# Expert network of a 16-layer model: token rows gathered tile by tile through an inverted map in place of 16 scatters before the tile loop

## The reference, cut to what matters

```python
x = x + _L2_ffn_ref(_layernorm(x, axis=-1), gate_w, gate_b, w1, b1, w2, b2)

def _L2_ffn_ref(x, gate_w, gate_b, w1, b1, w2, b2):     # 8 experts, 128 -> 512 -> 128, TOP_K = 2
    xt = x.reshape(b * s, h)
    probs = jax.nn.softmax(xt @ gate_w + gate_b, axis=-1)
    _, idx = jax.lax.top_k(probs, TOP_K)
    one_hot = jax.nn.one_hot(idx, NUM_EXPERTS, dtype=xt.dtype)
    mask = (one_hot.sum(axis=1) > 0).astype(xt.dtype)
    h1 = jax.nn.relu(jnp.einsum('th,ehf->etf', xt, w1) + b1[:, None, :])
    out_e = jnp.einsum('etf,efh->eth', h1, w2) + b2[:, None, :]
    out = jnp.einsum('eth,te->th', out_e, mask)
    return out.reshape(b, s, h)
```

## Time and profile before

| | |
|---|---|
| median of 3 runs | 2968.0 us (2967.19 to 2973.27) |
| the profiled execution's own time | 2966.24 us |
| its span, first to last instruction | 2964.7 us |
| busy: PE / DVE / ACT / POOL | 77% / 61% / 47% / 29% |
| mean granted clock of PE | 0.902 of full speed |
| DMA: all / POOL's own queue (q0) | 80.91 MB / 10.76 MB |
| the four expert stages, first to last instruction | 840.8 to 943.7, 1064.4 to 1166, 2315.7 to 2419, 2543.7 to 2646 us |

### The profile page before, as it was taken

One profiled execution on the slowest core, in us unless ns is written; L12 is line 12 of the kernel. 1 busy time (PEld: TensorE's weight loads), 2 busy tenths in 40 slices (PEclk: granted clock), 3 DMA queues, 4 the chain that ended last, 5 costly groups with the idle time before them and its releaser, 6 DMA issues. The chain is left out here.

```text
span 2964.7 us, 36677 instructions
## 1 busy us (share of the span) xinstructions
PE 2295.0 (77%) x12494; PEld 1086.6 (37%) x12494; DVE 1800.1 (61%) x3201; ACT 1393.2 (47%) x2324; POOL 858.3 (29%) x852
## 2 busy tenths in 40 slices
PE   6678879999757757777766787799997578577777
PEld 2222344544336226223222223445443452362232
DVE  5959565554525725885559595655455357259855
ACT  5535536555423434545455355366544234346454
POOL 3721151000224433651037211500001243336410
PEclk9998989999869878999989989999998687789999
DMA  3002000000021221000000020000000311210000
GB/s 140 0 18 67 10 1 9 1 1 1 1 96 52 71 96 36 0 0 1 9 8 0 27 60 7 1 9 1 1 1 1 99 60 59 96 36 0 1 2 14
DMA packets 58912, 80.91 MB, mean 27 GB/s; under 512 B 10784, under 2 KB 38944, under 8 KB 58464
## 3 DMA queue, kind: packets, MB, share of 16 engines
q1 hardware_dynamic: 49376, 63.81, 6.7%
q0 software_dynamic: 4992, 10.76, 1.1%
q10 hardware_dynamic: 4352, 3.94, 0.5%
HBM read 53.83 MB, written 26.08 MB: 27 GB/s over the span
## 5 line engine op out<-in xcount | busy, mean ns | idle before, releaser
L2227 ACT ACTIVATE L1b_pr<-ps,L1b_mneg 128x512 f32<-128x512 f32 x256 | 173.5, 682 | 191.3 <-DVE L1b_mneg L2268 191.3
L2266 DVE TENSOR_REDUCE L1b_m<-ps 128x2 f32<-128x1024 f32 x128 | 156.7, 1225 | 88.7 <-PE ps L2117 83.5
L96 ACT ACT_TABLE_LOAD x44 | 56.5, 1283 | 286.7 <-PEq L495 64.8
L1478 POOL TENSOR_TENSOR L0a_db<-L0a_du,L0a_bs 128x1024 f32<-128x1024 f32 x64 | 150.5, 2360 | 106.9 <-DVE L0a_du L1589 61.9
L1478 POOL TENSOR_TENSOR L3a_db<-L3a_du,L3a_bs 128x1024 f32<-128x1024 f32 x64 | 150.4, 2359 | 106.0 <-DVE L3a_du L1589 59.5
L1901 ACT ACTIVATE L0b_pt<-ps 128x1024 f32<-128x1024 f32 x128 | 125.6, 1022 | 97.3 <-PE ps L1801 97.2
L1989 DVE TENSOR_REDUCE L0b_mx<-ps 128x1 f32<-128x512 f32 x256 | 157.9, 682 | 20.3 <-PE ps L1788 17.7
L2292 DVE COPY L1b_prt<-ps 128x512 f32<-128x512 f32 x128 | 88.5, 691 | 126.4 <-PE ps L2130 126.1
L267 POOL CAST L1g_xc<-xn 128x512 bf16<-128x512 f32 x2 | 1.5, 731 | 558.5 <-DVE xn L142 558.5
L1606 DVE TENSOR_TENSOR_SCAN L3a_hs<-ps,L3a_db 128x1024 f32<-128x1024 f32 x64 | 146.0, 2282 | 5.3 <-ACT ps L1398 5.3
L1606 DVE TENSOR_TENSOR_SCAN L0a_hs<-ps,L0a_db 128x1024 f32<-128x1024 f32 x64 | 146.0, 2281 | 4.2 <-ACT ps L1398 4.2
(11 more groups left out here) (697 smaller groups left out, 5293.0 us busy)
## 6 DMA issues: line engine op xcount, KB each, us to landing
L2f_wall<-expert_dram SPq DMA_DIRECT2D x32, 256.0 KB, 5.6
L2g_wall<-expert_dram SPq DMA_DIRECT2D x32, 256.0 KB
weights<-w_dram SPq DMA_DIRECT2D x5, 941.5 KB, 14.1
L0b_qs<-stack_dram SPq DMA_DIRECT2D x32, 96.0 KB, 2.2
stack_dram<-L0b_cut SPq DMA_DIRECT2D x24, 128.0 KB, 2.1
L2b_qs<-stack_dram SPq DMA_DIRECT2D x32, 96.0 KB, 2.2
stack_dram<-L2b_cut SPq DMA_DIRECT2D x24, 128.0 KB, 2.2
L2f_xg<-slots SPq DMA_DIRECT2D x10, 288.0 KB, 4.7
```

Of the source, the lines that this page charges most:

```text
L1478: pool.tensor_tensor(db[:, n % DEEP, :, :], du[:, b, :, :], bcast(bs[:, n % DEEP, :], 1, 2), ALU.mult).then_inc(input_ready, 1)
L2227: act.activation(pr[:, s % 2, h, :], g.ps[:, 2 * (s % 2) + h, :], ACT.Exp, bias=mneg[:, s % 2, h:h + 1], accum_out=total[:, u % 2, t, h:h ...
L2266: dve.tensor_reduce(m[:, s % 2, :], g.ps[:, 2 * (s % 2):2 * (s % 2) + 2, :], AX.X, ALU.max).then_inc(max_raw, 1)
```

## The change

The token rows are stored once per pick in a DRAM tensor tokens, in the order 2 x token + pick, without the extra columns. DVE and PE invert the slot map: of each pick, DVE makes a 0/1 row over the 23 tiles (of_tile, from comparisons of slot_f with multiples of 128) and a 0/1 row over the 128 lanes of a tile (of_lane). PE multiplies the lane rows with the tile rows scaled by the two parts of the pick's number (ids_of: low = 2 x lane + pick, high = token tile), and so gets, for each slot, the number of the pick in it, 0 for an empty one. This is source. POOL gathers a tile's 128 rows from tokens with it: six gathers before the loop, then gather(n + 6) behind the scatter of tile n. The row numbers for the result scatter are source too, with a spare row added for empty slots, so they are ready before the loop. PE turns one tile at a time, two tiles ahead; ACT copies one tile at a time to xt, now three deep, behind choose.

```diff
-                part = SLOTS * WIDE
-                sp.dma_start(g.slots.rearrange("(p k) w -> p (k w)", p=P), wd[:, 0:part]).then_inc(g.rest_loaded, 16)
...
             @block.sync
-                sp.wait_ge(sent, 16 * 2 * NT)
-                for k in range(groups):
-                    a, z = GROUP * k * P, (GROUP * k + size(k)) * P
-                    sp.dma_start(xg[:, GROUP * k:GROUP * k + size(k), :], g.slots[a:z, :].rearrange("(t p) w -> p t w", p=P)).then_inc(group_in[k], 16)
+                for b in range(NB):
+                    sp.wait_ge(tok_in, b + 1)
+                    for k in range(2):
+                        rows = g.tokens[2 * b * T:2 * (b + 1) * T, :].rearrange("(t p k) c -> p t k c", p=P, k=2)
+                        sp.dma_start(rows[:, :, k, :], tok[:, b * KT:(b + 1) * KT, :]).then_inc(stored[b], 16)
...
             @block.tensor
+                for c in range(4):
+                    pe.wait_ge(lanes_ready, c + 1)
+                    for r in range(4 * c, 4 * c + 4):
+                        mm = pe.matmul(g.ps[:, 0, 0:2 * SLOTS], of_lane[:, r, :], ids_of[:, r, :, :].rearrange("p k n -> p (k n)"),
+                                       start=(r == 0), stop=(r == 2 * NT - 1))
+                mm.then_inc(named, 1)
...
+                def turn(n):
+                    pe.wait_ge(gathered[n % AHEAD], 16 * (n // AHEAD + 1))
+                    if n >= 2:
+                        pe.wait_ge(x_in, n - 1)
+                    pe.transpose(g.ps[:, 4 + n % 2, 0:P], xg[:, n, :], g.w("ident")).then_inc(x_turned, 1)
...
                 turn(0)
+                turn(1)
                 hidden_products(0)
                 for n in range(SLOTS):
-                    if n % GROUP == 0 and n // GROUP + 1 < groups:
-                        turn(n // GROUP + 1)
+                    if n + 2 < SLOTS:
+                        turn(n + 2)
...
             @block.scalar
-                    for k in range(2):
-                        act.activation(tok[:, k, b * KT:(b + 1) * KT, 0:P], g.ps[:, 6 + b, :].rearrange("p (t c) -> p t c", c=P), ACT.Copy).then_inc(tok_in, 1)
+                    act.activation(tok[:, b * KT:(b + 1) * KT, :], g.ps[:, 6 + b, :].rearrange("p (t c) -> p t c", c=P), ACT.Copy).then_inc(tok_in, 1)
...
+                for n in range(2, SLOTS):
+                    choose(n)
+                    x_copy(n)
...
             @block.vector
-                dve.tensor_scalar(slot[:, :], slot_f[:, :], -1.0, None, ALU.add).then_inc(slots_ready, 1)
+                dve.tensor_tensor(reached[:, :, :], bcast(slot_f[:, :], 2, SLOTS + 1), bcast(g.w("e2_step"), 1, 2 * NT), ALU.is_gt).then_inc(slots_ready, 1)
+                dve.wait_ge(slots_ready, 1)
+                dve.tensor_reduce(tile_f[:, :], reached[:, :, 1:SLOTS], AX.X, ALU.add).then_inc(slots_ready, 1)
+                dve.tensor_tensor(of_tile[:, :, :], reached[:, :, 0:SLOTS], reached[:, :, 1:SLOTS + 1], ALU.subtract).then_inc(slots_ready, 1)
+                dve.wait_ge(slots_ready, 2)
+                dve.scalar_tensor_tensor(out=lane[:, :], in0=tile_f[:, :], scalar=-float(P), in1=slot_f[:, :], op0=ALU.mult, op1=ALU.add).then_inc(slots_ready, 1)
+                dve.wait_ge(slots_ready, 3)
+                dve.tensor_tensor(ids_of[:, :, 0, :], of_tile[:, :, :], bcast(g.w("e2_low"), 2, SLOTS), ALU.mult).then_inc(slots_ready, 1)
+                dve.tensor_tensor(ids_of[:, :, 1, :], of_tile[:, :, :], bcast(g.w("e2_high"), 2, SLOTS), ALU.mult).then_inc(slots_ready, 1)
+                dve.wait_ge(slots_ready, 6)
+                for c in range(4):
+                    dve.tensor_tensor(of_lane[:, 4 * c:4 * c + 4, :], bcast(lane[:, 4 * c:4 * c + 4], 2, P), bcast(g.w("e2_lane"), 1, 4), ALU.is_equal).then_inc(lanes_ready, 1)
...
+                dve.wait_ge(named, 1)
+                dve.tensor_copy(id_f[:, :], names[:, 0, :]).then_inc(ids_ready, 1)
+                dve.wait_ge(ids_ready, 1)
+                dve.scalar_tensor_tensor(out=id_f[:, :], in0=names[:, 1, :], scalar=float(2 * P), in1=id_f[:, :], op0=ALU.mult, op1=ALU.add).then_inc(ids_ready, 1)
+                dve.wait_ge(ids_ready, 2)
+                dve.tensor_copy(source[:, :], id_f[:, :]).then_inc(source_ready, 1)
...
             @block.gpsimd
-                for b in range(NB):
-                    pool.wait_ge(tok_in, 2 * b + 2)
-                    for t in range(b * KT, (b + 1) * KT):
-                        for k in range(2):
-                            pool.indirect_dma_start(g.slots[:, :], bass.IndirectOffsetOnAxis(ap=slot[:, k * NT + t:k * NT + t + 1], axis=0),
-                                                    tok[:, k, t, :], None).then_inc(sent, 16)
+                def gather(n):
+                    pool.indirect_dma_start(xg[:, n, :], None, g.tokens[:, :],
+                                            bass.IndirectOffsetOnAxis(ap=source[:, n:n + 1], axis=0)).then_inc(gathered[n % AHEAD], 16)
+
+                pool.wait_ge(source_ready, 1)
+                for b in range(NB):
+                    pool.wait_ge(stored[b], 32)
+                for n in range(AHEAD):
+                    gather(n)
+                pool.wait_ge(rows_ready, 1)
                 for n in range(SLOTS):
-                    pool.wait_ge(rows_ready, n // GROUP + 1)
                     pool.wait_ge(y_in, n + 1)
                     pool.indirect_dma_start(g.rows[:, :], bass.IndirectOffsetOnAxis(ap=row[:, n:n + 1], axis=0),
                                             y[:, n, :], None).then_inc(returned, 16)
+                    if n + AHEAD < SLOTS:
+                        gather(n + AHEAD)
```

More of the change, by code:

```diff
@@ L437, in expert_ffn @@
     NT = NB * KT
-    GROUP = 4
+    AHEAD = 6
     with Stage(g, name) as st:
@@ L456, in expert_ffn @@
         slot_f = st.sb("slot_f", [P, 2 * NT])
-        slot = st.sb("slot", [P, 2 * NT], U32)
+        reached = st.sb("reached", [P, 2 * NT, SLOTS + 1])
+        tile_f = st.sb("tile_f", [P, 2 * NT])
+        lane = st.sb("lane", [P, 2 * NT])
+        of_tile = st.sb("of_tile", [P, 2 * NT, SLOTS])
+        ids_of = st.sb("ids_of", [P, 2 * NT, 2, SLOTS], BF16)
+        of_lane = st.sb("of_lane", [P, 2 * NT, P], BF16)
+        id_f = st.sb("id_f", [P, SLOTS])
+        source = st.sb("source", [P, SLOTS], U32)
         past = st.sb("past", [P, SLOTS, E])
@@ L559, in hidden_products @@
                         mm = pe.matmul(g.ps[:, n % 2, f * P:(f + 1) * P], wsel[:, n % 3, f * P:(f + 1) * P],
-                                       xt[:, n // GROUP % 2, n % GROUP, :], start=True, stop=True)
+                                       xt[:, n % 3, :], start=True, stop=True)
                     mm.then_inc(hidden, 1)
@@ L599, in _, with x_copy @@
                     act.activation(mask_t[:, b * KT:(b + 1) * KT, :], g.ps[0:E, 4 + b, :].rearrange("e (t c) -> e t c", c=P), ACT.Copy).then_inc(mask_in, 1)
-                def x_copy(k):
-                    act.wait_ge(x_turned, k + 1)
-                    if k >= 2:
-                        act.wait_ge(hidden, GROUP * (k - 1))
-                    act.activation(xt[:, k % 2, 0:size(k), :], g.ps[:, 4 + k % 2, 0:size(k) * P].rearrange("p (t c) -> p t c", c=P), ACT.Copy).then_inc(x_in, 1)
+                def x_copy(n):
+                    act.wait_ge(x_turned, n + 1)
+                    if n >= 3:
+                        act.wait_ge(hidden, n - 2)
+                    act.activation(xt[:, n % 3, :], g.ps[:, 4 + n % 2, 0:P], ACT.Copy).then_inc(x_in, 1)
                 def choose(n):
@@ L614, in _ @@
                 act.wait_ge(expert_in, 16 * 2 * E)
-                act.wait_ge(ids, 2)
+                act.wait_ge(bias_in, 1)
                 choose(0)
+                x_copy(0)
                 choose(1)
-                x_copy(0)
-                for n in range(SLOTS):
-                    if n + 2 < SLOTS:
-                        choose(n + 2)
-                    if n % GROUP == 0 and n // GROUP + 1 < groups:
-                        x_copy(n // GROUP + 1)
+                x_copy(1)
+                for n in range(2, SLOTS):
+                    choose(n)
+                    x_copy(n)
             @block.vector
@@ L686, in _ @@
                 dve.wait_ge(plan, 7)
-                dve.tensor_tensor(valid[:, :], g.w("e2_slot"), last[:, :], ALU.is_lt).then_inc(plan, 1)
-                dve.tensor_scalar(spare[:, :], g.w("e2_slot"), float(2 * NB * T), None, ALU.add).then_inc(plan, 1)
+                dve.tensor_tensor(valid[:, :], g.w("e2_slot"), last[:, :], ALU.is_ge).then_inc(plan, 1)
+                dve.wait_ge(plan, 8)
+                dve.tensor_tensor(spare[:, :], g.w("e2_spare"), valid[:, :], ALU.mult).then_inc(plan, 1)
                 dve.wait_ge(plan, 9)
-                dve.tensor_tensor(row_f[:, :], spare[:, :], valid[:, :], ALU.mult).then_inc(plan, 1)
-                dve.wait_ge(plan, 10)
-                dve.tensor_tensor(spare[:, :], spare[:, :], row_f[:, :], ALU.subtract).then_inc(rows_plan, 1)
```

(23 more changed lines are left out.)

48 lines of the change are left out of this document (17 added, 31 removed).

## The result

The kernel with the change took **2987.8 us** (median of 5 runs, 2986.0 to 2990.3), the kernel before 2968.05 (5 runs, 2967.2 to 2973.8). The ratio is 1.0062, 95% interval 1.0047 to 1.0076: slower by about 20 us, where 31 us faster were forecast.

The account below looks back on a forecast made before the run. It took TensorE to set the old loop (1.91 us a tile) and POOL the new (2.56). Per stage 16.6 us won in front less 8.9 in the loop, net 7.6; four stages 30.6 us, so 2937 us from 2968.0, range 2923 to 2964.

Parts of the forecast that it names:

- Plan: Before the loop: DVE's longer chain and 16 small products put the first gather 6.2 us after the old first scatter.
- stores: Before the loop: SP's 1 MB of row stores take 5.7 us, done about 860, before the first gather; cost 0.
- gather: On POOL: a gather costs 0.957 us like a scatter (ends 0.56 and 1.20), landing 1.35 us later.
- the first return: End of the front: first return goes out at 874.05 instead of 890.6, 16.6 us earlier.
- The loop: Tile loop: POOL's two jobs take 2.56 us a tile against 1.91, giving back 8.9 of the 16.6 us.
- A: POOL's queue: dearer gather, gain gone at 1.35 us, 2979 at 1.5; chance 0.07 above 1.38.
- B: Gather landing: 3.1 us instead of 1.35, 3.5 us lost a stage, 2951; chance 0.11 shared with A at 1.0 to 1.32.
- C: DMA queue: small transfers don't overlap, 2.3 us each, about 35 us longer a stage, 3109; chance 0.02.
- D: TensorE in the loop: waiting lowers its clock to half, 26 us more a stage, 3072; chance 0.02.
- a slower side of 0.11: Whole kernel: chance that the change makes it slower, from A above 1.38 (0.07), C (0.02) and D (0.02).

Follow-up runs that it names:

- run 12: Changed kernel with a copy of 128 x 256 (a rest of 0.4 us) on POOL behind every indirect DMA of the loop; 2987.7 us.
- run 1: Changed kernel with all 23 gathers issued before the first return instead of six; 3001.4 us, ratio 1.0105.
- run 4: Changed kernel with the gathers of tiles 6 to 22 replaced by plain 64 KB loads that SP issues (wrong rows); 2904.0 us.
- run 6: Changed kernel with the 17 gathers of the loop replaced by plain 64 KB loads without an index, issued by POOL; 2906.6 us.
- run 14: Changed kernel with a copy of 128 x 1024 (a rest of 1.05 us) on POOL behind every second gather only; 2979.7 us.
- run 2: Changed kernel with the gathers of tiles 6 to 22 left out, those tiles turning the first six tiles' rows again; 2902.9 us.
- run 15: Changed kernel with a copy of 128 x 256 on POOL behind each gather of the loop only; 2988.7 us, ratio 1.0065.

## Why the prediction was wrong, step by step

**Plan, stores, gather: right; the first return partly by luck.** First gather 6.5 us after reached (forecast 7.3), stores never waited for, a gather 0.97 us (0.957). The first gather was in use 2.8 us after its start (865.41 to 868.23), forecast 2.3. The first expert product stood 10.8 us after reached (forecast 11.6), and from there to the first return it took 6.5 us (5.7): the two misses of 0.8 us cancel in the 17.3 that was forecast and measured.

**The loop: this step failed.** As the prediction put it, "POOL now has two jobs a tile: 2 x 0.957 + 0.30 + 0.35 ... = 2.56 us. That is above 1.91, so POOL takes the bound over." Each term is right; pairs do start 2.56 apart while nothing stalls. The failure is in taking POOL's busy time and gaps for all that an indirect DMA costs. The sustained price was 1.53, so a pair is 3.07. First stage: 17 pairs took 51.7 us instead of 43.5, and the last five intervals 10.4 instead of 7.4, since the last tiles' results came late: 11.2 us over the forecast 68.3. The four stages (79.4, 77.9, 78.4, 79.3) are 315 us, against 273 forecast and 304 before. The row that should have warned stood in the trace: the only two kinds of stretch with indirect DMAs were 16 in a row with **TensorE idle**, and one in 1.91 us with it busy. Neither shows two in 2.56 us beside a busy TensorE, and the prediction carried the distance of the first into the second.

**Outside the stage.** The stages explain 11 of the 24 us between the two profiled executions; 4 are their distance from their medians. Of the 12.5 us outside the stages, 2.2 lie ahead of the first one, where nothing has stalled yet (it starts between 853.7 and 859.2 us in the 18 traces, in no order of the kernels), 5.5 between the first and the second, 1.1 between the second and the fourth and 3.7 behind the last. The clock in the layer behind differs too. The stretch 10 to 20 us after the last return, of the changed kernel, of run 12 and of the kernel before:

```profile
948.40:958.40 10.00, 7.74 (x15) 2.93 (x15) 2.07 (x3) 5.00 (x7) 6.96 (x2) 0.75 0.00 0
```

```profile
946.90:956.90 10.00, 7.64 (x24) 3.60 (x24) 3.43 (x5) 5.47 (x8) 6.96 (x2) 0.99 0.00 0
```

```profile
942.70:952.70 10.00, 7.65 (x25) 3.54 (x24) 3.53 (x6) 5.59 (x8) 6.96 (x2) 1.00 0.00 1
```

After the stalling loop TensorE has 0.75 of its clock, where the others have all of it, and its record has 15 products instead of 24 or 25. Span less the four stages is 2673 us in the changed kernel, 2662 in run 12 and 2661 before. In the seven traces without late signals it is 2658 to 2666 us, in the ten with them 2665 to 2677, and in run 1, where they end halfway into the stage, 2662. So it goes with the stalls; that they cause it, and that the clock is the way, was not tried by itself.

**Rivals.** A (a dearer gather, even at 1.35 us) was the nearest in kind and had the wrong place: the gather's row is cheap. The pair took 3.07 us instead of 2.56; put on the gather alone, these 0.51 us make it 1.47, beyond the 1.35 at which A turned the sign, and by A's 1.9 us a stage for each 0.1 us they make about 2976. A expected to see them in the gather's own row, where they are not. B did not occur. C said that something is paid for each small transfer, in series; that is nearer to what happened than the forecast, but it put it on the queue at 2.3 us and on small pieces of bytes, and runs 4 and 6 moved the same small pieces without harm. D: the clock did fall, to 0.88, in a loop with stalls, and TensorE waiting in run 12's loop at 71% busy kept 1.00; so waiting by itself did not bring it down. What the prediction named as its refutation, "POOL still waiting for y in the middle of the loop", is what the profile showed.

The range ended at 2964 because each rival was priced with rows for POOL or for landing, and none with a new interaction; a slower side of 0.11 was too small for a loop that asks an engine for a density that no row has shown.

## What to carry to other kernels

The busy time of a DMA issue on POOL is not its price. Before a loop gets more indirect DMAs, look for a stretch of the trace with that many per us beside the same engines at work; if there is none, bound the price by a distance that has been seen (here 1.91 us), not by the sum of busy and gap (1.27). When consumers start long after their producer's record ends, neither engine is the bound: look at what a third engine sends in that time. Here the price is by the instruction, so the change needed fewer indirect DMAs, not earlier ones: 46 a stage at 1.5 us behind a front of 6.5 make some 76 us, an estimate from these runs (the best of them, run 14, has 77.9), and the kernel before, with 39 of which 16 ran while TensorE stood still, takes 75.9. How much is at stake runs 2 and 4 show: with the 17 gathers of the loop gone from POOL, the same loop has stages of 61 us.

## What was not expected of the hardware

Late signals of TensorE under dense indirect DMAs of POOL: 2 to 4 us in the loop, 20 us with 24 in a row; in the kernels whose loop does not send them that closely DVE starts 0.0 to 0.4 us after the end. They depend on indirect DMAs alone (run 6: a plain one between them does nothing), not on direction, rows, bytes or semaphores that TensorE awaits. The Trainium skill, SBUF — State Buffer, section Who interferes with whom, says that DMA never contends with a compute engine and that TensorE and ScalarE wait on no one; it speaks there of the ports of SBUF. For bytes that land the runs agree (run 4: 61 us a stage). But TensorE's signals came up to 4.7 us late when POOL issued indirect DMAs closely, so it does not carry over to the time of a whole loop. No run here shows whether a port has a part in it.

And adding work made the kernel faster or no slower: 0.8 us more on POOL in each tile left the total as it was (run 12), and rests of 1.05 us behind every second gather took 8 us off in one run (run 14). The granted clock in the first stage's loop was higher with both, 1.00 and 0.97 instead of 0.88, but that doesn't explain it: run 15 also had 0.97 and was no faster (2988.7). After its first return POOL waited 0.3 us for results in the first stage of run 14, and 8.4 us in run 15's.
